# Cross-attention with a mixture FFN: projecting V inside the first attention pass, with score tiles ahead of the branch

## What is computed

```python
xn = layernorm(x)
q = (xn @ Wq + bq)  # 1024 x 16 heads x 8
k = (ctx @ Wk + bk) # 6404 x 16 heads x 8
v = (ctx @ Wv + bv)
attn = softmax(clip(q @ k.T * 8 ** -0.5, -1e4, 1e4))
x = x + (attn @ v) @ Wo + bo
y = layernorm(x)
main = gelu(y @ W1m + b1m) @ W2m + b2m
g = softmax(mean(y) @ w_gate + b_gate)     # the two best of 8 experts, weights normed to one
x = x + a * main + (1 - a) * sum(gate_w * expert(y))
```

## Time and profile before

| | us |
|---|---|
| median of 3 runs (794.29 to 796.16) | 794.51 |
| profiled execution | 795.02 |
| its span, first to last instruction | 793.2 |
| first exponential starts | 51.92 |
| last exponential starts | 736.1 |

### The profile page before, as it was taken

The page is one execution under the profiler, slowest core; times in us unless marked ns, Lnnn a source line. Parts: engine busy times, 40 slices in busy tenths (PEclk is TensorE's granted clock), DMA queues, the critical chain, the costliest instruction groups (busy, mean ns, idle before and its releaser), DMA issues.

```text
span 793.2 us, 13140 instructions
## 1 busy us (share of the span) xinstructions
PE 728.6 (92%) x5406; PEld 215.9 (27%) x5406; DVE 548.1 (69%) x760; ACT 724.9 (91%) x587; POOL 20.6 (3%) x36
## 2 busy tenths in 40 slices
PE   4988889999999999999899999999999989999898
PEld 2642222222222222222222222222222222222457
DVE  5634298789878978898788897897689882140220
ACT  3769999999999999999999999999999999999451
POOL 8000000000000000000000000000000000000000
PEclk9989999999999999999999999999999999999999
DMA  5258210011110000111100000111100000000010
GB/s 190 106 153 285 69 46 1 18 34 35 51 34 1 1 1 1 34 51 34 37 15 1 1 1 19 34 34 50 34 1 2 1 1 1 1 1 1 4 54 27
DMA packets 15324, 29.05 MB, mean 37 GB/s; under 512 B 2438, under 2 KB 5884, under 8 KB 15260
## 3 DMA queue, kind: packets, MB, share of 16 engines
q1 hardware_dynamic: 13562, 26.86, 11.0%
q10 hardware_dynamic: 1218, 0.64, 0.3%
q0 software_dynamic: 480, 0.66, 0.3%
HBM read 20.02 MB, written 8.13 MB: 35 GB/s over the span
## 4 chain that ended last, share of the span: by engine, by line
PE 53%; ACT 23%; issue 18%; DVE 3%; DMA 1%; POOLq 0%; SPq 0%; POOL 0%; ACTq 0%
PE po L1141 27%; ACT region_ctxT L516 22%; PE ps L1077 15%; PE ps L1222 2%; PE po L1232 1%; PE po L964 1%; PE ps L953 1%; DMA region_ctx<-in_ctx 1%; PE po L1127 1%; PE ps L941 1%; DVE xn L585 1%; PE po L1056 1%; DMA region_ctx<-in_w1e 0%; PE ps L1232 0%; PE ps L1072 0%
## 5 line engine op out<-in xcount | busy, mean ns | idle before, releaser
L516 ACT ACTIVATE region_ctxT<-ps 128x1536 f32<-128x1536 f32 x500 | 678.4, 1543 | 7.8 <-PE ps L1077 7.5
L1141 PE MATMUL po<-region_ctxT,v 128*9 128x512 f32 x2984 | 391.6, 597 | 0.5 <-ACT region_ctxT L516 0.5
L1077 PE MATMUL ps<-qst,region_k 32*128 32x512 f32 x1492 | 253.7, 495 | 42.3 <-ACT region_ctxT L516 41.5
L1077 PEld LDWEIGHTS ps<-qst,region_k 32*128 32x128 f32 x1492 | 97.2, 182 | 416.8 <-ACT region_ctxT L516 397.3
L766 DVE TENSOR_SCALAR region_kT<-po 128x512 f32<-128x512 f32 x108 | 74.1, 686 | 85.2 <-PE po L1077 85.2
L769 DVE SCALAR_TENSOR_TENSOR region_kT<-region_kT,po 128x512 f32<-128x512 f32 x108 | 73.4, 680 | 0.3
L1141 PEld LDWEIGHTS po<-region_ctxT,v 128*9 128x9 f32 x2984 | 44.3, 88 | 92.9 <-issue 89.4
L805 DVE SCALAR_TENSOR_TENSOR dres<-region_kT,dres 128x1024 f32<-128x1024 f32 x54 | 66.1, 1225 | 1.7
L802 DVE SCALAR_TENSOR_TENSOR dres<-region_kT,dres 128x1024 f32<-128x1024 f32 x54 | 65.8, 1218 | 0.1
L794 DVE SCALAR_TENSOR_TENSOR dres<-region_kT 128x1024 f32<-128x1024 f32 x54 | 65.7, 1218 | 0.0
L796 DVE SCALAR_TENSOR_TENSOR region_kT<-region_kT 128x1024 f32<-128x1024 f32 x54 | 65.7, 1217 | 0.0
(11 more groups left out here) (195 smaller groups left out, 304.3 us busy)
## 6 DMA issues: line engine op xcount, KB each, us to landing
region_k<-k_dram SPq DMA_DIRECT2D x40, 320.0 KB, 3.3
k_dram<-kparts SPq DMA_DIRECT2D x18, 320.0 KB, 4.3
qst<-q_dram SPq DMA_DIRECT2D x16, 128.0 KB
region_ctx<-in_ctx SPq DMA_DIRECT2D x2, 624.0 KB, 9.3
q_dram<-region_k SPq DMA_DIRECT2D x2, 512.0 KB, 2.7
k_dram<-kparts SPq DMA_DIRECT2D x2, 322.0 KB, 5.3
region_ctx<-in_ctx SPq DMA_DIRECT2D x1, 576.0 KB, 7.4
xres<-in_x SPq DMA_DIRECT2D x1, 512.0 KB, 4.4
```

The source lines that it names most:

```text
L516: act.activation(probs[:, t % NPR, :], ps[t % NSB][:, :], ACT.Exp, scale=ESCALE).then_inc(exp_ready, 1)
L1077: return mm(dst, kst[r, kt * P:(kt + 1) * P], qst[r, g, queries], start=True, stop=True)
L1141: last = mm(dst[QUAD * j:QUAD * j + V9, :], w, src, start=first, stop=last_one, skip_group_check=True)
```

## The change

**V inside the first pass.** Only V's chunks 0 and 1 are projected ahead of the loop, behind score tile 0. Chunks 2 to 12 become spare jobs of the first pass at tiles 2, 5, 8, ... 32 (`V_AT`), the bound matmuls at tiles 3 and 7, the flag's sum at 10, and the job that broadcasts the output bias and the FFN's bias rows at 12. All go into po1. VectorE takes their results (`take_job`), V's copies too, instead of ScalarE. Splits 0 to 3 of K stand among VectorE's range reductions, splits 4 to 9 behind V jobs 2 to 7 (`SPLIT_BEHIND`).

**Branch behind 14 tiles.** TensorE and ScalarE run the first 14 tiles (`NPRE`) before they read the flag. SyncE issues all of the first group's K stores and loads, and all q loads, before it.

**Probabilities.** Their four buffers leave the memory of the transposed context, which V's projection still reads: one is a tensor of its own, three lie where the context was.

**Layer norm.** GpSimd fills the row of ones of the transposed context and V's ones only behind the eighth scaling, and issues the small weights' DMAs (except Wv's) behind that. ScalarE loads the square root's table at the start and takes the root before the copies of chunk 1. The absolute value of q is made by VectorE, from q already scaled.

**Table.** `D_PLAN` has 27 rows as before, at other tiles: the first is at 37 to 56 instead of 26 to 48, and the last pass has three rows instead of two, its last values step at tile 499.

The diff, cut; the functions that only moved out of the branch with their text unchanged (`scores`, `score_tile`, most of `values_step`) are left out, and so are the general branch and `take_job`'s smaller cases:

```diff
@@ constants
-V_ORDER = [0, KCH // 2] + [c for c in range(1, VCH) if c != KCH // 2]
-BO_BANK = 3 + (KCH - 3) % 3
-FLAG_AHEAD = 3
-BOUND_AT = 4
+NPRE = 14
+V_AT = {c: 3 * c - 4 for c in range(2, VCH)}
+BOUND_TILES, GSUM_TILE, ROWS_TILE = (3, 7), 10, 12
 D_PLAN = [
-    (0, 49, (26, 28, 31, 33), (3, 1, 2, 0), 48),
-    (1, 49, (37, 40, 44, 50), (0, 1, 2, 3), 71),
+    (0, 49, (37, 39, 42, 44), (0, 2, 3, 1), 56),
+    (1, 49, (48, 51, 57, 60), (1, 2, 0, 3), 75),
...
-    (7, 48, (425, 428, 434, 473), (2, 3, 0, 1), 481),
+    (7, 48, (425, 428, 431, 477), (2, 3, 0, 1), 489),
+    (7, 47, (479, 481, 485, 488), (3, 1, 0, 2), 499),
 ]
 SPARE = sorted([(t, "score", GH * d + k) for d, (_, _, at, _, _) in enumerate(D_PLAN) for k, t in enumerate(at)]
-               + [(NORM_AT[p], "tokens", p) for p in range(NP - 1)])
+               + [(NORM_AT[p], "tokens", p) for p in range(NP - 1)] + [(t, "v", c) for c, t in V_AT.items()]
+               + [(t, "bound", n) for n, t in enumerate(BOUND_TILES)]
+               + [(GSUM_TILE, "gsum", 0), (ROWS_TILE, "rows", 0)])
+JOBS_PRE = sum(t < NPRE for t, _, _ in SPARE)
+JOBS_V = SPARE.index((V_AT[VCH - 1], "v", VCH - 1)) + 1
+
+SPLIT_BEHIND = {SPARE.index((V_AT[c], "v", c)): s for c, s in zip(range(2, VCH), range(4, NSEG))}
@@ probabilities
-        probs = region_ctxT[:, 0:NPR * CPT * BANK].rearrange("p (b n) -> p b n", b=NPR)
+        probs_own = sb("probs_own", [P, CPT * BANK])
+
+        def probs_of(t):
+
+            n = t % NPR
+            return probs_own[:, :] if n == 0 else region_ctx[:, (n - 1) * CPT * BANK:n * CPT * BANK]
@@ SyncE
             load_q(sp, 0)
-            store_k(sp, 0)
-            load_k(sp, 0, 0)
+            for s in range(NSEG):
+                store_k(sp, s)
+                if s != 1:
+                    load_k(sp, 0, max(s - 1, 0))
+            load_k(sp, 0, NSEG - 1)
+            load_k_tail(sp)
+            for g in range(1, NG):
+                load_q(sp, g)
             sp.wait_ge(flag_ready, 1)
             safe = sp.value_load(flag[0:1, 0:1], min_val=0, max_val=1)
             with sp.If(safe != 0):
-                for s in range(1, NSEG):
-                    store_k(sp, s)
-                    if s >= 2:
-                        load_k(sp, 0, s - 1)
-                load_k(sp, 0, NSEG - 1)
-                load_k_tail(sp)
-                for g in range(1, NG):
-                    load_q(sp, g)
@@ GpSimd
             pool.wait_ge(const_ready, 3)
-            pool.memset(region_ctxT[CK:CK + 1, :], 1.0).then_inc(pads_ready, 1)
-            pool.wait_ge(pads_ready, 1)
-            pool.memset(tailT[:, :], 0.0).then_inc(pads_ready, 1)
-            pool.wait_ge(pads_ready, 2)
-            pool.memset(ktail[:, :, :].bitcast(F32), 0.0).then_inc(pads_ready, 1)
             for dst, src in ((wv_sb[0:CK, :], wv), (wv_sb[CK:CK + 1, :], bv)):
                 pool.dma_start(dst, src).then_inc(wv_in, 16)
+            pool.memset(tailT[:, :], 0.0).then_inc(pads_ready, 1)
+            pool.wait_ge(pads_ready, 1)
+            pool.memset(ktail[:, :, :].bitcast(F32), 0.0).then_inc(pads_ready, 1)
+            pool.wait_ge(pads_ready, 2)
+            pool.wait_ge(xn_ready, QT)
+            pool.memset(region_ctxT[CK:CK + 1, :], 1.0).then_inc(pads_ready, 1)
+            pool.wait_ge(pads_ready, 3)
+            pool.memset(v9[:, :, :, D:V9], 1.0).then_inc(vones_ready, 1)
...
-            pool.memset(v9[:, :, :, D:V9], 1.0).then_inc(vones_ready, 1)
@@ ScalarE
+            act.wait_ge(scratch_ready, 1)
+            act.activation(scratch[:, :], scratch[:, :], ACT.Sqrt).then_inc(table_step, 1)
             evac_ctxT(act, 0)
-            evac_ctxT(act, 1)
             act.wait_ge(var_ready, 1)
             act.activation(rstd[:, 1, :], rstd[:, 0, :], ACT.Sqrt).then_inc(std_ready, 1)
+            evac_k(act, 0)
+            evac_ctxT(act, 1)
             evac_ctxT(act, 2)
...
-                act.activation(q_abs[:, n * BANK:(n + 1) * BANK], po[n][:, :], ACT.Abs, bias=bqc[:, 0:1]).then_inc(q_abs_ready, 1)
...
-            for nth in range(VCH):
-                if nth == VCH - FLAG_AHEAD:
-                    act.wait_ge(flag_ready, 1)
-                    safe = act.value_load(flag[0:1, 0:1], min_val=0, max_val=1)
-
-                    act.activation(scratch[:, :], ones[0:1, 0:1], ACT.Exp).then_inc(table_step, 1)
-                evac_v(act, nth)
-            with act.If(safe != 0):
-
-                for t in range(NT):
+            act.wait_ge(table_step, 1)
+            act.activation(scratch[:, :], ones[0:1, 0:1], ACT.Exp).then_inc(table_step, 1)
...
+            exponentials(range(NPRE))
+            act.wait_ge(flag_ready, 1)
+            safe = act.value_load(flag[0:1, 0:1], min_val=0, max_val=1)
+            with act.If(safe != 0):
+
+                exponentials(range(NPRE, NT))
@@ VectorE
+            def take_v(c, src):
+
+                n = min(4, FULL + 1 - 4 * c)
+                return v.tensor_copy(v9[:, 4 * c:4 * c + n, :, 0:D], src[:, 0:n * P].rearrange("p (t h d) -> p t h d", h=H, d=D))
...
             for c in range(KCH - 1):
-                if c == 1:
+                if c == 3:
                     split_q()
+                    link(v.scalar_tensor_tensor(q_abs, qT[:, :], -1.0, qT[:, :], ALU.mult, ALU.max))
                 range_k(c)
-                if c == 4:
-                    split_k(0, link)
+                if c in (2, 4, 7, 9):
+                    split_k((2, 4, 7, 9).index(c), link)
...
+            dve.wait_ge(v_psum, 1)
+            take_v(0, po[0]).then_inc(v_done, 1)
             link(range_k(KCH - 1))
...
+            dve.wait_ge(v_psum, 2)
+            take_v(1, po[1]).then_inc(v_done, 1)
...
+            def take_job(n, step):
+
+                _, kind, i = SPARE[n]
+                src = po[1]
+                dve.wait_ge(spare_psum, n + 1)
+                if kind == "v":
+                    take_v(i, src).then_inc(spare_taken, 1)
...
+                if n in SPLIT_BEHIND:
+                    split_k(SPLIT_BEHIND[n], step)
+
+            for n in range(JOBS_PRE):
+                take_job(n, link)
@@ TensorE
+            def spare_job(n):
+
+                t, kind, i = SPARE[n]
+                pe.wait_ge(v_done, 2)
+                if n:
+                    pe.wait_ge(spare_taken, n)
...
+                if kind == "v":
+                    last = project_v(i, po[1])
+                elif kind == "bound":
+                    pe.wait_ge(bounds_ready, 1)
+                    last = mm(po[1][0:2 * H, :], bounds[:, :], q_abs[:, i * BANK:(i + 1) * BANK], start=True, stop=True)
...
+            score_tile(0)
+            pe.wait_ge(q_ready, NHALF)
+            project_v(0, po[0]).then_inc(v_psum, 1)
+            project_v(1, po[1]).then_inc(v_psum, 1)
+            pe.wait_ge(k_ready, KCH)
+            score_tile(1)
...
+            score_tiles(range(NPRE))
+            pe.wait_ge(flag_ready, 1)
+            safe = pe.value_load(flag[0:1, 0:1], min_val=0, max_val=1)
+            with pe.If(safe != 0):
+                score_tiles(range(NPRE, NT))
```

More of the change, by code:

```diff
@@ L978, in _ @@
             ctx_transpose(4)
-            project_k(2)
+            project_k(3)
             pe.wait_ge(wts_in, 48)
@@ new lines, in _, with scores @@
+            seen = set()
+            def scores(dst, p, kt, j):
+                g, half = PASSES[p]
+                queries = slice(half * BANK, (half + 1) * BANK)
+                if ("q", g) not in seen:
+                    seen.add(("q", g))
+                    pe.wait_ge(qst_in[g], 16 * GH)
+                if kt == FULL:
+                    if "tail" not in seen:
+                        seen.add("tail")
+                        pe.wait_ge(ktail_ready, GH)
+                    return mm(dst, ktail[:, g, :], qst[:, g, queries], start=True, stop=True)
+                if (g, kt // SEG_T) not in seen:
+                    seen.add((g, kt // SEG_T))
+                    pe.wait_ge(kst_in[kt // SEG_T], 16 * (g + 1))
+                r = slice(QUAD * j, QUAD * (j + 1))
+                return mm(dst, kst[r, kt * P:(kt + 1) * P], qst[r, g, queries], start=True, stop=True)
@@ L1150, in _, with score_tiles @@
+            score_tile(0)
[4 more added lines that the diff above has]
+            score_tile(1)
+            def score_tiles(tiles):
+                for t in tiles:
                     if t + NSB < NT:
@@ L1179, in _ @@
             with pe.Else():
+                pe.wait_ge(exp_ready, NPRE)
+                for n in range(JOBS_PRE, JOBS_V):
+                    spare_job(n)
                 with pe.Fori(0, H) as h:
```

309 lines of the change are left out of this document (142 added, 167 removed), and 41 rows, old and new, of the table D_PLAN.

## The result

The changed kernel takes 802.24 us (median of 5 runs, 801.31 to 804.27), the kernel before 794.51 (5 runs, 793.87 to 796.16): a ratio of 1.0098, 95% interval 1.0076 to 1.0120. It is slower. The profiled execution took 804.27 us, 2.0 above its median, with a span of 802.5.

What follows compares the result with a forecast made beforehand. ScalarE's exponentials were taken to pace the kernel, 1.33 us a tile, TensorE having 0.165 us slack. Terms -8.0 + 3.0 + 9.2 + 1.0 + 0.2 + 1.0 = +6.4 us gave 801 us, range 795 to 806.

Steps and rivals of the forecast that it cites:

- first scores: Start of the first score matmul: 43.4 us against 51.38, -8.0 us, bounds -5.8 and -8.9.
- from there to iteration 2: First scores to third iteration: 9.0 us instead of 6.0, V's copies standing behind K splits; +3.0 us, bounds +2 and +5.
- iterations 2 to 35, with the flag: First pass: TensorE paces 34 iterations with V's jobs, 55.6 us against 46.4, +9.2; the flag's +1.0 comes on top.
- rest of the loop: Table of tiles: one VectorE step added to the last pass, +0.2 us; other stretches as before.
- end behind the last exponential: Values at tile 499 stand behind the tail's; eight value matmuls take 0.98 us with nothing hiding them: +1.0 us.
- The chain to the first scores: Before the loop: q's second part 3.7 us earlier, passed on whole by the DMA chain; V and flag's 4.3 us hold goes.
- Rival 1: First pass: V hides in TensorE's gaps and exponentials keep the pace; 789.5 us, 8%.
- rival 2: Early lead kept: V copies taken as soon as scores run, jobs at 0.96 us, register load covered; 794.7 us, 14%.
- Rival 4: Low clock lasts beyond 52.4 into the V jobs, each us costing about 0.5: up to +3, 804 us; 12%.
- The flag: Register load at the branch, about 1.0 us, paid in full where TensorE paces: +1.0 us, 0 to +2.
- Rival 3: Before first scores: GpSimd's fills or descriptor writing block the q split, taking say 2.2 us of the lead; 803.2 us, 18%.
- The signs named: Expected trace: first scores at 43 to 44, first values near 51, iteration 2 near 52.4, tile 36 at 106 to 109.

Runs made afterwards that it cites:

- d_end: The changed kernel with the tiles of the table's last row two to four earlier and the last two of the row before two earlier: 804.29 us, 1.0104.
- flag_late: The changed kernel with 36 instead of 14 tiles ahead of the flag's register loads: 801.52 us, 1.0083.
- warm: The changed kernel with 56 dummy matmuls on TensorE in the wait for K: 801.27 us, 1.0086.
- v_in_wait: The changed kernel with V chunks 0 to 11 projected while TensorE waits for K and copied by ScalarE, only chunk 12 in the loop: 791.22 us, 0.9960.
- chain_v6: The changed kernel with faster q and K transfers, V chunks 0 to 5 projected in the wait, and the exponential's table loaded early: 786.15 us, 0.9886.
- best_a: chain_v6 with 36 tiles ahead of the branch, V chunk 6 at tile 0, and eight dummy matmuls behind score tile 1: 781.78 us, 0.9842.
- ln_chain: The kernel before with the change's layer-norm part and faster q and K transfers, V still projected whole ahead of the loop: 790.63 us, 0.9947.

## Why the prediction came out right

Forecast 801, measured 802.24, the sign and the range right. The main mechanism, V's jobs paced by TensorE, is right too; that the total came so close is partly luck, as the steps show. From the two profiled executions:

| step | predicted | measured |
|---|---|---|
| first scores | -8.0 | -4.6 (46.78 against 51.38) |
| from there to iteration 2 | +3.0 | +3.4 (9.43 against 6.03) |
| iterations 2 to 35, with the flag | +9.2 + 1.0 | +11.3 (57.70 against 46.42) |
| rest of the loop | +0.2 | -2.1 |
| end behind the last exponential | +1.0 | +1.3 |
| sum | +6.4 | +9.3 |

**The chain to the first scores** failed in one link. "The DMA chain behind it is unchanged, so it moves whole" is wrong: q's second part was ready at 22.3 (forecast 22.1), but the q store then met the small weights' DMAs, which the change had moved there, and took 3.4 us longer. In the other runs of the changed front (d_end, flag_late) it took 2.0 and 1.2 us longer and the first scores are at 44.8 and 44.1, so some 2 us belong to this execution, which also lies 2.0 us above its median. There the term is -6.5 and -7.3. In this execution only the 4.3 us came that V and the flag had held, and 0.3 of the 3.7.

**To iteration 2**: the size was right, and so was the near tie of the two paths (50.9 for V's copies, 50.7 for TensorE). VectorE's second copy:

```profile
53.51 0.69 DVE L645 COPY v<-po 128x512 f32<-128x512 f32 x1
```

Split 3 waited until 49.04 for its store, and this copy ended at 54.20. TensorE came at 54.38 and did not wait for it: in this execution its own path at the low clock, two V chunks in 3.72 us and then a wait for an exponential, was the later. In warm the copy was, by 0.25 us.

**The loop** carried the result. A V job was put at 1.06 us and took 1.09, and TensorE paced the stretch; v_in_wait against warm confirms it. Rival 1, V in TensorE's gaps, falls with that, and rival 2, which needs jobs at 0.96 and an early third iteration. The smaller jobs were put too high: a bound job took 0.86 us (67.94 to 70.21, less 0.43 and 0.98) and was put at 1.1. The sum and the row job took 0.17 and 0.51, put at 0.35 and 0.75.

**Rival 4 was part of the truth.** The low clock lasted to about 62, 6 us into iterations 2 and 3, and not only to their start. I gave it 12% as an alternative; it belonged in the sum. The two iterations took 7.60 us (56.21 to 63.81). At clock 1.00 they need 0.43 + 1.09 + 0.98 = 2.50 and, like iteration 7 with the other bound job, 2.27. So the low clock cost 2.8 us, close to the half microsecond for each that rival 4 names. Chain_v6 against best_a agrees: 2.7 us in tiles 4 to 14, with 5.9 us of low clock in them.

**The flag** was mis-sized: 1.0 in the sum, 0.2 at most by the trace. In the earlier trace rows 1.0 us is the time from the flag to TensorE's next matmul; TensorE itself stood idle for 0.50 of it, as that row says. Here scores for two tiles were already out when the register was read. So within the loop's line the missing 2.8 us of clock were partly made up by the flag's 0.8 and by 0.6 for the jobs, and the line came out 1.1 too low.

**Rival 3**, GpSimd in the way of the q split, did not happen: cast and subtraction take 0.69 and 1.22, as before. One cast of a K split took 0.75 instead of 0.49, at 24.66, off the path.

**The table**: the end's 1.0 was right. VectorE's first copy behind the last exponential comes 1.0 us later than before; the other 0.3 of the 1.3 lie further on, in work that was not changed. d_end shows that it isn't had back by moving the row by two tiles. The rest of the loop gained 2.1 where I had a loss of 0.2; 1.2 of it lies in tiles 50 to 75 (35.08 us, before 36.28), where the table's rows stand elsewhere. Which of the moved rows makes it was not tried.

**The signs named** show the same. Tile 36 started at 111.64 and not at 106 to 109, and tiles 4 to 36 were 1.71 us apart and not 1.55 to 1.65. From tile 14 on, at clock 1.00, they were 1.54 apart. Against the forecast the lead was 3.4 us short in this execution and the loop 1.1 us long; 2.3 us of unforeseen gain in the rest of the loop hid half of that.

## What to carry to other kernels

Before work is moved into a loop, add up the time per iteration of the engine that gets it: a slack of 0.165 us a tile cannot hold a job of 1.09 us in every third tile, and the engine that was second sets the pace for as long as the jobs last. Work belongs into a wait while there is one (v_in_wait), and a shorter wait is worth nothing until the work is movable (ln_chain): the two pay together (chain_v6, best_a). When a step starts earlier, ask what it now shares the DMA engines with, and look at their share during the chain: behind a share of 0.14, in a stretch that everything waits for, lay 10 us. Where the clock is low at the start of the added work, price that in too.
